# Gated loads, queries spread ahead of the first keys, and high casts moved off VectorE in a perceiver block

## The reference

```python
q = x @ Wq                       # 16 heads of 64
k, v = jnp.split(context @ Wkv, 2, axis=-1)
k = concat(null_key, heads(k)); v = concat(null_value, heads(v))
q, k = jnp.tanh(q), jnp.tanh(k)
attn = softmax(einsum('bhid,bhjd->bhij', q, k) * 64 ** -0.5)
out = einsum('bhij,bhjd->bhid', attn, v) @ Wout + bout
```

## Time and profile before

| | us |
|---|---|
| median of 3 runs | 207.89 (207.77 to 207.90) |
| profiled execution, its own time | 207.87 |
| its span, first to last instruction | 206.1 |
| TensorE busy | 193.1 (94%) |
| VectorE busy | 143.2 (69%) |
| ScalarE busy | 118.7 (58%) |
| GpSimd busy | 35.1 (17%) |

### The profile page before, as it was taken

How to read it: one execution, slowest core, us unless ns; L and a number is a source line. 1 busy time by engine, 2 the same in 40 slices (tenths; PEclk the granted TensorE clock), 3 DMA queues, 4 the chain that set the end, 5 groups by cost and what they waited for, 6 DMA issues and landing times.

```text
span 206.1 us, 4175 instructions
## 1 busy us (share of the span) xinstructions
PE 193.1 (94%) x1642; PEld 148.0 (72%) x1644; DVE 143.2 (69%) x253; ACT 118.7 (58%) x223; POOL 35.1 (17%) x43
## 2 busy tenths in 40 slices
PE   7797999899999999999999999999998799999991
PEld 2597789788998899988998767857685244645560
DVE  2359989889897999989978699634872927214313
ACT  2479789878977798778977645006532322322300
POOL 2196004031050220401302000020401300000001
PEclk9999999999999999999999999999999999999999
DMA  6996397992002030010000896999999500000000
GB/s 200 368 333 123 112 248 231 303 319 102 3 13 92 0 102 3 0 54 0 5 0 2 266 388 180 380 378 379 379 378 378 161 0 3 0 0 0 3 2 25
DMA packets 19668, 30.46 MB, mean 148 GB/s; under 512 B 1969, under 2 KB 13634, under 8 KB 19650
## 3 DMA queue, kind: packets, MB, share of 16 engines
q1 hardware_dynamic: 19506, 30.14, 44.2%
q10 hardware_dynamic: 144, 0.07, 0.1%
HBM read 30.07 MB, written 0.13 MB: 147 GB/s over the span
## 4 chain that ended last, share of the span: by engine, by line
PE 59%; issue 21%; DVE 12%; DMA 3%; ACT 2%; POOL 2%; SPq 1%; POOLq 0%; ACTq 0%
PE ps L1054 36%; PE ps L1088 6%; DVE keys L765 4%; DMA mixT<-in_Wq 3%; PE ps L1130 2%; PE ps L1144 2%; DVE ex_l L725 2%; DVE ex_sum L787 1%; PE ps L1277 1%; DVE q_two L756 1%; PE ps L1244 1%; PE ps L1116 1%; PE ps L1325 1%; PE ps L1154 1%; PE ps L1260 1%
## 5 line engine op out<-in xcount | busy, mean ns | idle before, releaser
L765 DVE SCALAR_TENSOR_TENSOR keys<-ps,keys 64x512 f16<-64x512 f32 x64 | 44.1, 689 | 2.2 <-ACT keys L584 0.2
L584 ACT ACTIVATE keys<-ps 64x512 f16<-64x512 f32 x64 | 37.9, 592 | 1.8
L1054 PE MATMUL ps<-ctxT_h,w_k_h 128*128 128x256 f32 x128 | 37.8, 295 | 0.5 <-DVE keys L765 0.5
L1054 PE MATMUL ps<-ctxT_h,w_k_l 128*128 128x256 f32 x128 | 36.2, 282 | 0.0
L1054 PE MATMUL ps<-ctxT_l,w_k_h 128*128 128x256 f32 x128 | 36.1, 282 | 0.0
L725 DVE TENSOR_TENSOR ex_l<-ps,ex_h 128x512 fp32r<-128x512 f32 x32 | 22.0, 687 | 9.1 <-ACT ps L607 9.0
L606 ACT ACTIVATE ex_h<-ps 128x512 fp32r<-128x512 f32 x32 | 19.0, 595 | 15.0 <-PE ps L1088 14.8
L1054 PE MATMUL ps<-ex_h,ctx_h 128*128 128x512 f32 x64 | 25.4, 398 | 0.0
L1054 PE MATMUL ps<-ex_l,ctx_h 128*128 128x512 f32 x64 | 25.1, 392 | 0.0
L1054 PEld LDWEIGHTS ps<-ctxT_h,w_k_h 128*128 128x128 f32 x128 | 24.4, 191 | 1.0 <-issue 0.9
L1054 PE MATMUL ps<-ex_h,ctx_l 128*128 128x512 f32 x64 | 24.9, 389 | 0.0
(11 more groups left out here) (193 smaller groups left out, 263.8 us busy)
## 6 DMA issues: line engine op xcount, KB each, us to landing
w<-in_fc1T SPq DMA_DIRECT2D x8, 1024.0 KB, 12.5
w<-in_fc SPq DMA_DIRECT2D x8, 1024.0 KB, 12.3
stage_t<-in_ctxT SPq DMA_DIRECT2D x8, 256.0 KB, 3.0
stage_n<-in_ctx SPq DMA_DIRECT2D x8, 256.0 KB, 2.6
mixT<-in_Wq SPq DMA_DIRECT2D x2, 512.0 KB, 4.7
w_k_stage<-in_Wk SPq DMA_DIRECT2D x4, 256.0 KB, 6.3
w_v<-in_Wkv SPq DMA_DIRECT2D x1, 1024.0 KB, 7.3
w_out<-in_Wout SPq DMA_DIRECT2D x1, 1024.0 KB, 10.2
```

The costliest lines, as they stand in the source:

```text
L584: nc.scalar.activation(keys[rows, u % 2, PK * i:PK * (i + 1), r], full[rows].rearrange("p (j n) -> p j n", j=PK), ACT.Copy, scale=UNIT).th ...
L765: V.scalar_tensor_tensor(out=keys[other, u % 2, PK * i:PK * (i + 1), r], in0=ps[mine, K_BANK + kp % 2].rearrange("p (j n) -> p j n", j=PK) ...
L1054: last = MM(dst, lhs[i], rhs[j], start=start and m == 0, stop=stop and m == len(parts) - 1)
```

## The change

Five edits. (1) SP waits between issues: the second half of Wq is issued when x has landed, key weights 1 when the first half of Wq has landed, and so on, up to null_k and all that follows when key weights 2 have landed. (2) TensorE spreads queries 0 and 1 (8 transposes) before project_keys(0) and not after it. (3) The high parts of queries 0 and 1 are made on ScalarE, before keys_tanh(0); VectorE's low parts of queries 0 and 1 come together before low_keys(0) and (1). (4) high_ctxT(n) for n >= 2 and (5) high_ctx(n) for n >= 1 move from VectorE to GpSimd, with the same waits on TensorE's progress.

```diff
@@ SP
             load_ctxT(0)
+            sp.wait_ge(ld_x, 16)
             sp.dma_start(w_q[:, 1], a["Wq"][1]).then_inc(ld_wq[1], 16)
-            for i in range(1, G * KT):
-                sp.dma_start(w_k_piece(w_k_stage, i), a["Wk"][i]).then_inc(ld_wk[i], 16)
+            sp.wait_ge(ld_wq[0], 16)
+            load_wk(1)
+            sp.wait_ge(ld_wk[0], 16)
+            load_wk(2)
+            sp.wait_ge(ld_ctxT[0], 16)
+            load_wk(3)
+            sp.wait_ge(ld_wq[1], 16)
             load_ctxT(1)
+            sp.wait_ge(ld_wk[1], 16)
             load_ctx(0)
+            sp.wait_ge(ld_wk[2], 16)
             sp.dma_start(null_k[:], a["null_k"]).then_inc(ld_null, 16)
@@ GpSimd
             def high_ctxT(n):
                 pool.wait_ge(ld_ctxT[n], 16)
+                if n >= 2:
+                    pool.wait_ge(k_psum, G * KT * (n - 1))
                 nc.gpsimd.tensor_copy(ctxT_h[:, n % 2], stage_t[:, n % 2]).then_inc(ctxT_high, 1)
             def high_ctx(n):
                 pool.wait_ge(ld_ctx[n], 16)
+                if n >= 2:
+                    pool.wait_ge(mix_done, G * KT * (n - 1))
                 nc.gpsimd.tensor_copy(ctx_h[:, n % 2], stage_n[:, n % 2]).then_inc(ctx_high, 1)
...
                     for n in range(1, B * NC):
                         if n + 1 < B * NC:
+                            high_ctxT(n + 1)
                             low_ctxT(n + 1)
+                        high_ctx(n)
                         low_ctx(n)
@@ ScalarE
                 query_tanh(m)
+            high_queries(0)
+            high_queries(1)
             keys_tanh(0)
@@ VectorE
             def low_queries(m):
-                if m >= 2:
-                    dve.wait_ge(q_high, m - 1)
+                dve.wait_ge(q_high, m + 1)
...
-            for m in range(2):
-                high_queries(m)
-                low_queries(m)
-                low_keys(m)
+            low_queries(0)
+            low_queries(1)
+            low_keys(0)
+            low_keys(1)
...
                     low_keys(kp)
-                    if g == G - 1 and n + 2 < B * NC and kp == KT * u + AHEAD:
-                        high_ctxT(n + 2)
...
-                if g == G - 1 and n + 1 < B * NC:
-                    high_ctx(n + 1)
@@ TensorE
             project_queries(1)
-            project_keys(0)
             spread_queries(0)
             spread_queries(1)
+            project_keys(0)
             project_keys(1)
```

More of the change, by code:

```diff
@@ L406, in _, with load_wk @@
             sp.dma_start(x0[:], a["x"]).then_inc(ld_x, 16)
+            def load_wk(i):
+                sp.dma_start(w_k_piece(w_k_stage, i), a["Wk"][i]).then_inc(ld_wk[i], 16)
             sp.dma_start(w_q[:, 0], a["Wq"][0]).then_inc(ld_wq[0], 16)
-            sp.dma_start(w_k_piece(w_k_stage, 0), a["Wk"][0]).then_inc(ld_wk[0], 16)
+            load_wk(0)
             load_ctxT(0)
+            sp.wait_ge(ld_x, 16)
             sp.dma_start(w_q[:, 1], a["Wq"][1]).then_inc(ld_wq[1], 16)
-            for i in range(1, G * KT):
-                sp.dma_start(w_k_piece(w_k_stage, i), a["Wk"][i]).then_inc(ld_wk[i], 16)
+            sp.wait_ge(ld_wq[0], 16)
[5 more added lines that the diff above has]
+            sp.wait_ge(ld_wq[1], 16)
             load_ctxT(1)
+            sp.wait_ge(ld_wk[1], 16)
             load_ctx(0)
+            sp.wait_ge(ld_wk[2], 16)
             sp.dma_start(null_k[:], a["null_k"]).then_inc(ld_null, 16)
```

## The result

The changed kernel took 206.44 us in the median of 4 runs (206.31 to 206.91), the kernel before 207.89 (207.77 to 208.10): a ratio of 0.9931, 95% interval 0.9907 to 0.9955. It is faster, by 1.45 us; the forecast was 1.8, to 206.1. The forecast's own range, 205.4 to 206.8, holds it, and so does it hold the 206.5 of the rival in which the loads land no sooner, which is the nearer of the two.

The account below looks back on a forecast made before the run. TensorE bounds the kernel without a gap from unit 3's scores at 37.57 us, so only the prologue before them can pay. Order -0.83, casts -0.53 and gated loads -0.4 sum to -1.76 us: 206.1 us, range 205.4 to 206.8.

Parts of the forecast that it names:

- the rival in which the loads land no sooner: Prologue loads: Wq's second half lands at 8.6 us or later, only order and casts pay; 206.5 us, chance 0.26.
- Order of the prologue, -0.83 us: Prologue: with transposes first and high parts on ScalarE, keys 4 start at 20.40 us instead of 21.23.
- the price of transposing first: TensorE prologue: eight transposes ahead of keys 0 make the first tanh of keys 0.9 us later.
- The hidden cost on ScalarE: ScalarE prologue: two new high parts, 1.09 us together, run during keys 0, leaving 0.4 us before the tanh of keys.
- High casts, -0.53 us: VectorE, 26.16 to 33.59 us: moving context's high casts to GpSimd frees unit 2's low exponentials; later pairs are worth nothing.
- Gated loads, -0.4 us: Prologue loads: waits between issues bring the landing of Wq's second half from 8.6 to 8.2 us.
- L: Landing time of the second half of Wq; it moves every step of the prologue chain by its own amount.
- the doubt: Load queue: descriptors are consumed in ring order, so later loads take nothing from Wq; the sum would stay -1.36 us.
- 262 against 368 GB/s: Loads, 4.6 to 8.6 us: 1,024 KB landed at 262 while engines moved 368, read as loads issued behind also moving.
- the 8.2 to 8.3 named as a sign of being right: TensorE prologue: the second query projection starts at 8.2 to 8.3 us if the forecast is right.
- GpSimd does not slow VectorE in the steady stretch: Rival, steady stretch: GpSimd's added work slows VectorE, up to 215.7 us; chance 0.05.
- The gates did not starve the prologue: Rival, prologue: gated key weights 1 or L would come too late, at 12.8 or 10.4 us; chance 0.02.

Follow-up runs that it names:

- keys-first run: Changed kernel with keys 0 projected before the transposes of queries 0 and 1, high parts still on ScalarE: 206.43 us, ratio 0.9926.
- the best kernel: Changed kernel with Wq's second half issued right behind its first and ScalarE's table loaded at the start: 205.78 us, ratio 0.9902.
- its twin without gates: Wq's second half issued right behind its first, table loaded at the start, but no waits between loads, against the changed kernel: 206.20 us, ratio 0.9913.
- the one with the late table load: Changed kernel with Wq's second half issued right behind its first, ScalarE's table load standing behind its first wait: 206.42 us, ratio 0.9914.

## Why the prediction was right, and where it was not

*What bounds.* Right: everything behind the scores of unit 3 merely shifted; from there to the scores of unit 14 it took 73.33 us before and 73.27 after, by the chain. Expert 0's weights, which now go out sooner and were put down at nothing, cost nothing: from the scores of unit 3 to the end of the span it is 168.5 us before and 168.4 after.

*Order of the prologue, -0.83 us.* The mechanism was right, the size is 0.74. Keys 4 start at P + 11.81; before it was 12.55. The hidden cost on ScalarE was hidden, with 0.64 us to spare. Part of the story was wrong: I put down 0.9 us as the price of transposing first. It is no price at all, as the keys-first run shows (0.1 us the other way); had I asked what ScalarE does between its first tanh and the exponentials, I would have seen that it does the same either way.

*High casts, -0.53 us.* Measured 0.55, and alone 0.54 in the mean span (205.97 to 205.43). The pairs behind the first are worth nothing, as said. On GpSimd the first cast waited for its load (21.85 us, my 20), with as much room as expected.

*Gated loads, -0.4 us.* This step failed. Its size is at most a half of that (0.2 us, barely clear of nothing), and its mechanism is not in the traces. The sentence that L "moves every step" was right, and so was the doubt, which hung on the ring order that the Trainium skill's "DMA: Bandwidth & Descriptors" states: from the landing of key weights 0 on, the traces with and without gates agree with it. What I had taken for the cost of company, 262 against 368 GB/s, is no measure of it: before, key weights 0 landed at 6.72, so their 256 KB took 2.1 of the 4.0 us, and the 768 KB behind them 1.9, about 410 GB/s with all the company there. The slow part is there with the gates too (4.51 to 6.10 us, 1.6); what makes it slow is open. The gates did what they say, and to each load: key weights 1 took 4.2 us from issue to landing and not 6.2, having waited in SP's row and not in the queue. For a microsecond the DMA engines moved less than before (135 GB/s where it was 272), and made it up; the windows of the changed kernel, the last two columns being the DMA share and GB/s:

```profile
4.00:5.00 1.00, 1.00 (x5) 0.55 (x4) 0.34 (x2) 0.00 (x0) 0.51 (x1) 1.00 0.62 135
5.00:6.00 1.00, 1.00 (x4) 0.43 (x3) 0.42 (x1) 0.00 (x0) 0.05 (x1) 1.00 1.06 410
```

So that P stands 0.58 earlier in the changed kernel's first profile than before is for the most part luck of these two executions, and that it fell near the 8.2 to 8.3 named as a sign of being right bears out nothing. What does move P is the load's place: two places forward in the queue, with gates, it was 7.5.

*The sum.* Order and casts together 1.28 us shorter in distance, 1.36 forecast. What is left of the 1.45 us measured, 0.17, is within the scatter of P and the 0.2 that the gates may bring. The forecast's 0.3 us too much is in the main the gates' term.

*Rivals.* GpSimd does not slow VectorE in the steady stretch: low keys took 688 ns, as before. The gates did not starve the prologue: key weights 1 landed at 8.7, ahead of need.

## What to carry to other kernels

Compare two traces by the distance between two instructions on the chain, not by their times from the start: a load's landing scattered by up to a microsecond here with nothing changed ahead of it, more than any single edit was worth, and one profile of each kernel would have credited that luck to the edit. Before crediting a relieved engine, carry its chain to the point where the bound engine runs without a gap; only what stands ahead of that point counts. To bring a load forward, move it ahead in its queue: that brought 0.6 us here, and holding back what stands behind it 0.2 at best.

## What the runs showed of the hardware that was not expected

GpSimd and VectorE do get in each other's way in one case. A cast on GpSimd that began together with a VectorE subtraction of two SBUF operands (VectorE's row: 9.46 us, 0.69) took 1.15 us where it otherwise takes 0.61:

```profile
9.47 1.15 POOL L490 CAST w_k_h<-w_k_stage 128x512 fp32r<-128x512 f32 x1 [4.41 <-DMA w_k_stage<-in_Wk]
```

That is in the best kernel; in its twin without gates the same pair met at 10.01 us and the cast took 1.11. In the one with the late table load the same pair overlapped the other way: VectorE's subtraction took 0.98 and not 0.69, and GpSimd's next 1.60 and not 1.28 (rows above). VectorE's instructions of the steady stretch read one operand from PSUM and show none of this (low keys 688 ns, 689 before). It is the case that the Trainium skill, "GPSIMD Engine Reference", "Specifications", names (two SBUF inputs); these traces agree.

TensorE's first matmuls ran at two speeds. The two warm-up matmuls ahead of the first projection took 0.59 us in the profiled execution of before and 1.06 in that of the changed kernel, and the first projection ended at 7.23 us in the one and 7.89 in the other, though the granted clock is 1.00 in every window of the first 9 us of both. It is no mark of either kernel: the changed kernel without its gates has 0.59, the kernel before with them 1.06. What decides between the two is open. In one execution, that of the twin without gates, it made P later than the load.
